# Routing of rows to experts placed in the second attention's loop, expert weights turned beside the first experts' gated sums, norms by tile

## The reference

```python
x = x + _L0_gnn_ref(_layernorm(x), adj, W, a)                 # attention with leaky scores, softmax over neighbours, elu
x = x + _L0_ffn_ref(_layernorm(x)[None], ...)[0]              # 4 experts, gates from an attention over 524288 edges
x = x + _L1_gnn_ref(_layernorm(x), adj, W1, b1, W2, Ww, bw)   # softmax over neighbours of u[i] + v[j]
x = x + _L1_ffn_ref(_layernorm(x)[None], router_w, w1, w2, w3)[0]
```

```python
logits = flat @ router_w.T                 # 8 experts
probs = jax.nn.softmax(logits, axis=-1)
topk_probs, topk_idx = jax.lax.top_k(probs, 2)
topk_probs = topk_probs / (jnp.sum(topk_probs, axis=-1, keepdims=True) + 1e-09)
h = jax.nn.silu(h1) * h3                   # h1 = flat @ w1[e].T, h3 = flat @ w3[e].T, hidden size 341
out = jnp.einsum('ne,nec->nc', gates, y)   # y = h @ w2[e].T
```

## Time and profile before

| | |
|---|---|
| median of 3 runs | 4628.69 us (4625.09 to 4630.29) |
| profiled execution, its own time | 4628.36 us |
| its span in the trace | 4626.7 us |
| TensorE matmul busy | 3072.4 us (66%) |
| VectorE busy | 2684.8 us (58%) |
| ScalarE busy | 1413.4 us (31%) |
| GpSimd (POOL) busy | 1163.7 us (25%) |
| mean granted TensorE clock | 0.86 |

### The profile page before, as it was taken

The page is one execution under the profiler, slowest core; times in us unless marked ns, Lnnn a source line. Parts: engine busy times, 40 slices in busy tenths (PEclk is TensorE's granted clock), DMA queues, the critical chain, the costliest instruction groups (busy, mean ns, idle before and its releaser), DMA issues. The chain is left out here.

```text
span 4626.7 us, 59364 instructions
## 1 busy us (share of the span) xinstructions
PE 3072.4 (66%) x17374; PEld 1968.3 (43%) x17374; DVE 2684.8 (58%) x5008; ACT 1413.4 (31%) x2187; POOL 1163.7 (25%) x1158
## 2 busy tenths in 40 slices
PE   0002889537999999999905884000599999652995
PEld 0002778424555555555504553000355555341663
DVE  8998878746888888888872222148421222340333
ACT  0000034204777777777701553000100000010221
POOL 0000050006777500000003777610000000065442
PEclk9999998757999999999956997555599999856997
DMA  1003700115877877787612222321133333312335
GB/s 73 0 0 135 311 1 0 55 38 195 292 281 276 288 277 286 276 294 277 224 37 34 73 69 57 87 34 47 33 100 99 100 100 100 89 62 78 126 126 178
DMA packets 259370, 601.91 MB, mean 130 GB/s; under 512 B 73132, under 2 KB 99891, under 8 KB 258425
## 3 DMA queue, kind: packets, MB, share of 16 engines
q1 hardware_dynamic: 185184, 489.72, 31.2%
q10 hardware_dynamic: 39256, 88.65, 4.9%
q0 software_dynamic: 34880, 22.97, 2.6%
HBM read 402.86 MB, written 177.26 MB: 125 GB/s over the span
## 5 line engine op out<-in xcount | busy, mean ns | idle before, releaser
L1629 PE MATMUL at_out<-at_pt,g_H 128*128 128x512 f32 x2048 | 998.1, 610 | 54.3 <-DVE at_turned L1548 46.1
L1470 ACT ACTIVATE at_rl<-at_qrow,at_less,at_steep 128x512 f32<-128x512 f32 x1024 | 746.5, 805 | 9.0 <-DVE at_turned L1548 9.0
L1846 PE MATMUL at_out<-at_parts,at_a 128*128 128x387 bf16 x4096 | 679.5, 329 | 55.1 <-issue 55.1
L1555 DVE SCALAR_TENSOR_TENSOR at_pt<-at_rl,at_turned 128x1024 f32<-128x1024 f32 x512 | 608.5, 1217 | 15.7 <-ACT at_rl L1470 15.7
L1846 PEld LDWEIGHTS at_out<-at_parts,at_a 128*128 128x128 fp8e4 x4096 | 399.6, 98 | 334.7 <-issue 58.1
L1548 DVE CAST at_turned<-at_tp 128x1024 uint8<-128x1024 f32 x322 | 393.4, 1222 | 176.7 <-PE at_tp L1620 174.8
L1629 PEld LDWEIGHTS at_out<-at_pt,g_H 128*128 128x128 f32 x2048 | 350.1, 191 | 310.1 <-issue 302.6
L1620 PEld LDWEIGHTS at_tp<-at_identS,at_adj 128*128 128x128 fp8e4 x4128 | 275.4, 98 | 303.7 <-issue 303.7
L795 POOL DMA_INDIRECT rec<-at_part x304 | 375.2, 1234 | 103.5 <-issue 86.3
L955 POOL DMA_INDIRECT runs_GT<-tab,runs_RC x352 | 338.4, 961 | 116.4 <-issue 105.2
L1620 PE MATMUL at_tp<-at_identS,at_adj 128*128 128x128 bf16 x4128 | 316.6, 220 | 9.4 <-DMA at_adj<-in_adj_dram 8.7
(11 more groups left out here) (577 smaller groups left out, 4691.4 us busy)
## 6 DMA issues: line engine op xcount, KB each, us to landing
at_adj<-in_adj_dram SPq DMA_DIRECT2D x516, 512.0 KB
adjT<-at_turned ACTq DMA_DIRECT2D x128, 512.0 KB, 5.2
at_a<-adjT SPq DMA_DIRECT2D x128, 512.0 KB
runs<-count_clear SPq DMA_DIRECT2D x131, 384.0 KB
ex_WB<-top_weights SPq DMA_DIRECT2D x42, 533.0 KB, 3.0
y<-runs_YS ACTq DMA_DIRECT2D x65, 256.0 KB
f_YB<-y SPq DMA_DIRECT2D x16, 1024.0 KB, 6.9
ex_SL<-slots SPq DMA_DIRECT2D x42, 260.0 KB
```

Source lines behind the costliest of these rows:

```text
L1470: ins = nc.scalar.activation(RL[v % NBUF][:, k, :], qrow[:], ACT.Relu, bias=less[:], scale=steep[:, u:u + 1])
L1555: nc.vector.scalar_tensor_tensor(out=PT[v % NBUF][:], in0=RL[v % NBUF][:], scalar=1.0, in1=AT[v // VC % NAT][:, 2 * (v % VC):2 * (v % VC) ...
L1629: ins = nc.tensor.matmul(OUT[:], H[:, u, :], PT[v % NBUF][:, k, :], start=(u == 0), stop=(u == T - 1))
L1846: ins = nc.tensor.matmul(OUT[:, g, x, 0:3 * D1], ones[c % NBUF][:, j, x * P:(x + 1) * P], parts[:, u].rearrange("p k d -> p (k d)"), start ...
```

## The change

`norm_rows` becomes a norm by tile: one statistics instruction per tile, small operations on the 64 (or, in the loop, 4) means and variances, then one subtract-and-multiply per tile, which releases TensorE after every fourth. The old one stays as `norm_whole` for the gates of the first experts. `project_l0` starts the statistics of a quarter of x when it lands and computes the scores of group g-1 behind the transposes of group g; in all three projections ScalarE copies out of PSUM. The loop at the end of the first attention is written out 64 times.

`attend_levels` becomes `attend_route`: the routing of a block of four tiles follows its `finish` on VectorE, TensorE's parts of it (`turn`, `score`, `rank`) stand inside the next block's sums at u = 32, 37 and 56, ScalarE takes square root, exponential and two copies, and POOL scatters eight times per block from two copies of Y. `route_l1` is gone. The weights are turned in `combine_l0` by TensorE and ScalarE and stored in DRAM (`wts`), from where the experts load them.

```diff
+def norm_rows(nc, dve, step, X, Y, st6, small, rsqrt_ready, sqrt_done, width, rows_ok, beside=None):
...
+    for t in range(T):
+        if beside is not None:
+            beside(t)
+        ins = nc.vector.bn_stats(st6[:, t, :], X[:, t, :])
+    step(ins)
...
+    dve.sem_inc(rsqrt_ready, 1)
...
+    dve.wait_ge(sqrt_done, 1)
+    step(nc.vector.reciprocal(rstd, rstd))
+    for t in range(T):
+        ins = nc.vector.tensor_scalar(Y[:, t, :], X[:, t, :], mean[:, t:t + 1], rstd[:, t:t + 1], ALU.subtract, ALU.mult)
+        if t % 4 == 3:
+            ins.then_inc(rows_ok, 1)
...
-                with dve.Fori(0, T) as t:
-                    row = prop[:, bass.ds(t + RT, 1), :].rearrange("p a d -> p (a d)")
-                    nc.vector.scalar_tensor_tensor(out=row, in0=mean[:], scalar=todo[:, bass.ds(t + RT, 1)], in1=row, op0=ALU.mult, op1=ALU.add)
+                for t in range(T):
+                    ins = nc.vector.scalar_tensor_tensor(out=prop[:, t + RT, :], in0=mean[:], scalar=todo[:, t + RT:t + RT + 1], in1=prop[:, t + RT, :], op0=ALU.mult, op1=ALU.add)
...
+                def body(l, i, q):
+                    for g in range(GB):
+                        pool.wait_ge(dest_ok, q * GB + g + 1)
...
+                        pool.wait_ge(y2_ok, q * GB + g + 1)
...
+                        for k in range(2):
+                            for x in range(QT):
+                                pool.indirect_dma_start(slots, bass.IndirectOffsetOnAxis(ap=dest[g][:, k, x:x + 1], axis=0),
+                                                        Y[g][k][:, x, :], None).then_inc(scat[g], 16)
+                        pool.wait_ge(scat[g], q * (32 * QT) + 32 * QT)
+                        pool.sem_inc(sent, 1)
...
+                def sums(b, g, route_last):
+                    for c in range(C):
...
+                        if c == 0:
+                            pe.wait_ge(fin, b * QT + QT)
...
+                            pe.wait_ge(routed, b + 1)
...
+                        for j in range(JB):
+                            u = c * JB + j
+                            if route_last and u == TURN:
+                                turn(b - 1, 1 - g)
+                            if route_last and u == SCORE:
+                                score(b - 1, 1 - g)
+                            if route_last and u == RANK:
+                                rank(b - 1, 1 - g)
+                            for x in range(QT):
+                                ins = nc.tensor.matmul(OUT[:, g, x, 0:3 * D1], ones[c % NBUF][:, j, x * P:(x + 1) * P],
+                                                       parts[:, u].rearrange("p k d -> p (k d)"), start=(u == 0), stop=(u == T - 1))
...
+                    end = l * NQ + (NQ - 1)
+                    sums(end, 1, True)
+                    turn(end, 1)
+                    score(end, 1)
+                    rank(end, 1)
...
+                nested(sp, None, body)
+                sp.wait_ge(count_ok, 1)
+                sp.wait_ge(all_sent, 1)
+                for e in range(NE):
+                    n = sp.value_load(cnti[0:1, 0, e:e + 1], min_val=0, max_val=N)
+                    sp.dma_start(slots[bass.ds(n + e * REGION, BANK), :].rearrange("(p q) c -> p q c", q=4), zero[:]).then_inc(zeroed, 16)
...
 def combine_l0(nc, ident, X, gates, y, YB, y_in, w1, w2, w3, wts):
...
+                for e in range(NE1):
+                    b = e % 2
+                    act.wait_ge(turned, e + 1)
+                    if e >= 2:
+                        act.wait_ge(w_out[b], 16 * (e // 2))
+                    for s in range(2):
+                        nc.scalar.copy(wrow[b][:, s * HID:(s + 1) * HID], PS[:, b, s, 0:HID])
+                    for k, (o, n) in enumerate(parts):
+                        ins = nc.scalar.copy(wrow[b][0:n, 2 * HID + k * D:2 * HID + (k + 1) * D], PS[0:n, b, 2, k * D:(k + 1) * D])
+                    ins.then_inc(w_copied, 1)
+                    act.wait_ge(w_copied, e + 1)
+                    act.dma_start(wts[e], wrow[b][:]).then_inc(w_out[b], 16)
+                    if e + 2 < NE1:
+                        fetch(e + 2)
```

More of the change, by code:

```diff
@@ L72, in sems, with norm_whole @@
         return [self.sem(n) for n in names]
-def norm_rows(nc, dve, step, X, Y, work, small, rsqrt_ready, sqrt_done, width):
+def norm_whole(nc, dve, step, X, Y, work, small, rsqrt_ready, sqrt_done, width):
     T = X.shape[1]
@@ L200, in _, with scores @@
                 nc.tensor.matmul(PS[:, 7, 128:130], WT[:], a2[:], start=True, stop=True).then_inc(wa_ok, 1)
-                pe.wait_ge(xn_ok, 1)
                 pe.wait_ge(wa_out, 1)
+                def scores(g):
+                    pe.wait_ge(xt_out, g + 1)
+                    for k in range(4):
+                        ins = nc.tensor.matmul(PS[:, 6, 2 * (4 * g + k):2 * (4 * g + k) + 2], XT[:, 4 * g + k, :], wa[:], start=True, stop=True)
+                    ins.then_inc(d_ok, 1)
                 for g in range(G):
+                    pe.wait_ge(xn_ok, g + 1)
                     if g >= 2:
@@ L208, in _ @@
                     ins.then_inc(xt_ok, 1)
[L209 to L212, removed]
+                    if g:
+                        scores(g - 1)
+                scores(G - 1)
                 pe.wait_ge(scol_ok, 1)
@@ L261, in _ @@
                 step(nc.vector.scalar_tensor_tensor(out=X[:], in0=E[:], scalar=-1.0, in1=X[:], op0=ALU.add, op1=ALU.add))
[L262 to L267, removed]
+                norm_rows(nc, dve, step, X, Y, st6, small, var_ok, sqrt_ok, D, y_ok)
                 dve.wait_ge(h_ok, 1)
@@ L1790, in attend_levels @@
     GB = 2
+    NE = router_w.shape[0]
+    REGION = N + BANK
+    NJ = tiles.shape[2]
+    TURN, SCORE, RANK = 32, 37, 56
     assert NQ % GB == 0 and C % NBUF == 0
@@ L1800, in attend_levels @@
         st = ph.sbuf("st", [P, 4])
+        Y = [[ph.sbuf(f"Y{g}_{k}", [P, QT, D + 2]) for k in range(2)] for g in range(GB)]
+        FT = ph.sbuf("FT", [P, QT, D])
+        rw = ph.sbuf("rw", [NE, D])
+        rwT = ph.sbuf("rwT", [D, NE])
+        st6 = ph.sbuf("st6", [P, QT, 6])
+        small = ph.sbuf("small", [P, 4, QT])
+        ids = ph.sbuf("ids", [P, T], I32)
+        full = ph.sbuf("full", [P, P])
+        less = ph.sbuf("less", [P, P])
+        upto = ph.sbuf("upto", [P, P])
+        first = ph.sbuf("first", [P, QT, NE])
+        again = ph.sbuf("again", [P, NE, QT])
+        region = ph.sbuf("region", [P, NE])
+        base = ph.sbuf("base", [P, NE])
+        tile_no = ph.sbuf("tile_no", [1, NJ])
+        prob = ph.sbuf("prob", [P, QT, NE])
+        rest = ph.sbuf("rest", [P, QT, NE])
+        sel = [ph.sbuf(f"sel{k}", [P, QT, NE]) for k in range(2)]
+        pre = ph.sbuf("pre", [P, QT, NE])
+        pick = ph.sbuf("pick", [P, 2, QT, NE])
+        both = ph.sbuf("both", [P, NE, QT])
+        count = ph.sbuf("count", [P, NE, QT])
+        place = ph.sbuf("place", [P, NE, QT])
+        slot = ph.sbuf("slot", [P, NE, QT])
+        best = ph.sbuf("best", [P, 2, QT])
+        free = ph.sbuf("free", [P, QT])
+        destF = ph.sbuf("destF", [P, 2, QT])
+        dest = [ph.sbuf(f"dest{g}", [P, 2, QT], I32) for g in range(GB)]
+        zero = ph.sbuf("zero", [P, 4, D + 2])
+        cnt = ph.sbuf("cnt", [1, 3, NE])
+        cnti = ph.sbuf("cnti", [1, 2, NE], I32)
+        past = ph.sbuf("past", [1, 2, NJ, NE])
+        row = ph.sbuf("row", [1, 3, NJ])
         OUT = ph.psum("out", [P, GB, QT, BANK])
@@ L1851, in _, with turn, score @@
-                pe.sem_inc(used, NBUF)
-                nested(pe, lambda l: (pe.wait_ge(split_ok, l + 1), pe.sem_inc(passed, 1)), body)
+                def turn(b, g):
+                    pe.wait_ge(y_ok, b + 1)
+                    pe.sem_inc(passed, 1)
+                    for x in range(QT):
+                        ins = nc.tensor.transpose(OUT[:, g, 0, x * P:(x + 1) * P], Y[g][0][:, x, 0:D], ident[:])
+                    ins.then_inc(turned, 1)
+                def score(b, g):
+                    pe.wait_ge(t_out, b + 1)
+                    pe.sem_inc(passed, 1)
+                    for x in range(QT):
+                        ins = nc.tensor.matmul(OUT[:, g, 1, x * NE:(x + 1) * NE], FT[:, x, :], rwT[:], start=True, stop=True)
+                    ins.then_inc(l_ok, 1)
@@ L2567, in _ @@
+                for b in range(2):
+                    act.wait_ge(w_out[b], 16 * (NE1 // 2))
             @block.sync
```

562 lines of the change are left out of this document (242 added, 320 removed).

## The result

Faster: 4340.91 us (median of 4 runs, 4340.62 to 4340.99) against 4627.53 for the kernel before on the same chip; ratio 0.9379, 95% interval 0.9367 to 0.9391. Forecast: 4348, range 4328 to 4390. The profiled execution took 4340.99, its span is 4339.4 where it was 4626.7: 287.3 less.

| step | from, to (before; after) | forecast | measured |
|---|---|---|---|
| first projection | 928.01, 1049.19; 930.20, 994.34 | -57.5 | -57.0 |
| straight tail of the first attention | 2314.18, 2347.20; 2258.06, 2276.64 | -15.4 | -14.4 |
| second projection, to its table's store | 2382.08, 2473.32; 2310.60, 2372.90 | -29.1 | -28.9 |
| gated sums, to the next stage | 3096.95, 3177.97; 2996.87, 3078.08 | 0 | +0.2 |
| third projection | 3184.72, 3269.89; 3084.64, 3140.71 | -29.1 | -29.1 |

What follows compares the result with a forecast made beforehand. No engine bounds the whole kernel: it is a row of stages with barriers, so savings on a stage's chain count. -57.5 -29.1 -29.1 -15.4 -180.8 +3.2 +28.5 = -280.2 from 4628.4 gives 4348 us, range 4328 to 4390.

Steps and rivals of the forecast that it cites:

- Norms by tile, the projections: Three norms with their projections: TensorE starts earlier and the first projection's rounds shorten; -57.5, -29.1 and -29.1 us.
- Rival (d): Norm by tile: rounds at 3.62 us, not 2.49, in all three projections because one engine copies; +54, 4402 us; chance 0.05.
- Straight tail: End of the first attention: 64 unrolled operations at 0.253 us take 16.3 us against 31.7; -15.4 us.
- Weights in the sums: Expert weights turned in the gated sums: 5.6 us per expert on ScalarE, 45 in all, covered by 79.9 us; cost 0.
- rival (a): Gated sums: the weights outlast the sums, deciding from 9.5 us per expert; +36 at 1.69 per load, 4384 us; chance 0.10.
- Start of the second attention: Before the second attention's sums: VectorE waits for POOL's twelve constants; +3.2 us, bounds 0.2 and 4.5.
- Routing inside the loop: Second attention's sums: TensorE pays 16 instructions at 0.118 us, 1.9 per block, fifteen blocks; +28.5 us, no wait.
- Rival (b): Second attention's loop: TensorE pays the cold price per block, 4.4 us; +38, 4386 us; chance 0.08.
- Rival (c): Second attention's loop: VectorE's chain (`y_ok` or the copy) is late by 4 us beyond its slack; +60, 4408 us; chance 0.07.
- POOL beside VectorE: Routing in the loop: four tensor_scalar could each wait one scatter, 0.96 us; 3.8 on the chain, nothing paid.
- rival (e): Second attention's loop: slower than before, VectorE's chain so late that TensorE stands in every block, eating 280 us; chance 0.03.
- Tail: Last matmul to the experts' first load: 54 us in place of 234.8; -180.8 us, bounds 51 to 62 if POOL's drain is longer.

## Why the prediction was right

- **Norms by tile, the projections.** They came out as worked out: -57.0, -28.9, -29.1 for -57.5, -29.1, -29.1. The order's share in the first was shown by a run (15 us; 18 was taken for order and copy together). Rival (d), rounds of 3.62 because one engine copies, has 2.45 in the trace against it.
- **Straight tail.** 0.264 us per operation, not 0.253: -14.4 instead of -15.4.
- **Weights in the sums.** The step "5.6 us x 8 = 45 [...] Cost 0" had the right cost and the wrong size: 8.9 us per expert in the middle of the stage. The row of a 64 KB load gave the issue (there six in 3.3 to 4.1 us, 0.55 to 0.68 each, where 0.43 was taken), but the landing was taken as hidden behind the other buffer, and it sets the pace. The sum had no term for the DMA engines, which the sums' own loads and the weights fill together. The last store landed some 9 us before VectorE ended (3060.68 and a median of 6.7 to land, against 3076.9), where the forecast left 32; that nothing was paid is in part luck. The point from which rival (a) decides was right, and a run that crossed it paid 12.3.
- **Start of the second attention.** +2.8 for +3.2, through VectorE's wait; when that was taken away, ScalarE's wait for the same constants kept it.
- **Routing inside the loop.** The step "0.118 each: 1.9 us. Fifteen blocks: +28.5" was mis-sized: 1.57, +23.5; issued again, the same instructions cost 1.94. Rival (b), 4.4, is excluded. Against it the prediction could have said more: that mixed float32 and byte streams are "nowhere in this trace" is a wrong reading, since the first attention of the kernel before mixes float32 matmuls (L1629) with transposes of adjacency bytes (L1620) at a granted clock of 1.00 from 1500 to 2300. Rival (c) is excluded here by the timeline and by the run that asks 4 us earlier without a wait; when they are asked 8 us earlier, each wait is paid in full, with the lower clock on top.
- **POOL beside VectorE** (rival (e), and the Trainium skill's page "SBUF — State Buffer", section "Who interferes with whom", by which a tensor_scalar in a two-port mode could wait for a whole scatter). `finish` took 12.2 us in the first block, where no scatter runs, and up to 12.5 beside scatters (12.2 to 12.4 before), its 64 tensor_scalar 201 to 216 ns (212 to 216 before), the scatters 952 to 1087. Nothing of the kind shows in these operations of one column; the wider ones of the normalising do not fall beside scatters here.
- **Tail.** Step by step within 1.2 us. One thing was wrong and cost nothing, since SP's stores end later: "the drain now ends at about 50" took 9.2 us from the earlier trace rows; it took 1.37 and ended at 41.7.
- **Not forecast:** the experts' -2.9, by most of the traces through where the rows of a buffer lie, though the median of the run that moved Z did not confirm it. It (2.9) and the block's price (5.0) give more than the 7 us between 4348 and 4341; the straight tail's missing 1.0 takes some of it back.

## What to carry to other kernels

Work that has room beside a bound engine costs what it puts on that engine, here 1.6 us per block for 220 us of a separate stage; ask for its data with some slack behind the time at which they are ready (0.8 us was enough here), since a wait costs its length and, where the clock falls behind it, 1.5 to 2.7 us more in this loop. Before work is called hidden, count its landing times and the bytes of all that moves beside it, not only its issues. Behind a change, read every mark to the end: the next gain (9 us here) was a wait that stood ahead of stores which did not need it.

## What the runs showed of the hardware

- TensorE at 1.00 that stood 3.4 us in each block was granted 0.50 until 3 to 5.5 us behind the end of 8 of these 15 stalls; with no stall (the changed kernel) it stayed at 1.00 for over 640 us, from 3250 to the last matmul.
- POOL's drain behind scatters took 1.37 us here and 9.2 before, with 128 scatters in both. Here POOL had waited for each block's eight to land, before only for all of them at the end; whether that is the cause wasn't tried.
- The DMA engines were full (a busy share of 1.03, 356 GB/s) while two queues moved 1 MB loads and an expert's weights in and out, and each expert's loads then set the pace at 8.9 us; with the 1 MB loads over, the same work took 4.4 to 5.1.
- Loads of 1 MB in rows of 512 bytes: with the SBUF rows of both F and Z 32 or 160 bytes past a multiple of 512, SP's queue took 3.13 to 3.15 us for each of the last; with only F's off, 2.9 to 3.0 for F's last; on a multiple 2.28 to 2.32 (one execution excepted). The Trainium skill's page "DMA: Bandwidth & Descriptors", section "How a descriptor splits into AXI transactions", says that a descriptor which does not start on a multiple of 256 bytes begins with a transaction from the boundary below, whose unused bytes still cost; it says so of what is read, and here it is the side written that lies off. The direction agrees. Worked out from its counts (an estimate), rows 32 past would cost 17 beats for 16 and rows 160 past 21 for 16, where the runs show the same 37% for both; by its count of transactions it would be 3 for 2 in both.
